# Where a turn computes the score rows of the next image: keys half or logits half

## The chip, the cores and the metric

The kernel runs on one core of a Trainium2 chip. The metric is the time of one execution on the device in microseconds (us), as the median of several runs. The engines are called TensorE (PE in the rows, its weight loads PEld), VectorE (DVE), ScalarE (ACT), GpSimd (POOL) and SyncE (SP, which issues all DMAs).

## What is computed

Eight images of 256 channels and 1024 pixels pass two attention layers. Layer 0 has 32 channels of queries and keys and no scale; layer 1 has group norm (32 groups), 256 channels and a projection:

```python
# layer 0, for each image, x: 256 x 1024
q = Wq x + bq; k = Wk x + bk; v = Wv x + bv            # q, k: 32 x 1024
x = gamma * v softmax(q^T k)^T + x
# layer 1
h = group_norm(x); q, k, v = q_w h + q_b, k_w h + k_b, v_w h + v_b
x = x + proj_w (v softmax(q^T k / 16)^T) + proj_b
```

## The kernel before

**Three matmuls for one.** Most operands are kept as a high and a low part, both in the type fp32r, and a product is high x high, high x low and low x high (`three`, L595, whose matmuls have the lines L596 to L598). ScalarE or GpSimd makes the high part, DVE or GpSimd the low part.

**Tiles.** An image has eight tiles of 128 pixels. In layer 0 a tile is handled twice. A *scores* tile (`scores`, L600, matmuls at L606) has query pixels in the partitions: DVE takes the maximum of its rows (L1058), and ScalarE the exponential with the row's sum (L841, in place). After all eight of an image ScalarE takes the logarithm of the sums (`log_sums`, L844), DVE makes -max - log(sum) of it, split in two (`shifts`, L1081), TensorE turns that into two rows (`move_shift`, L630), and ScalarE copies these to two extra rows of the query operand (`shift_rows`, L848). A *keys* tile (`keys`, L609, matmuls at L616) then has key pixels in the partitions and comes out shifted, so that one exponential (L817) gives finished probabilities; keys tile 0 waits for the shift rows. In layer 1 a *logits* tile (`logits`, L619) has its maximum, exponential, inverse sum and scaling in one pass (L1060, L1061, L820, L1067, L834). Each probability tile is split (ScalarE L831 or L834, DVE L1075 or L1078) and goes into a value product two steps later: twelve matmuls of 512 columns into four banks of PSUM slots 2 and 3 (`values`, L747). The value product needs the values' high and low parts. Those of layer 1 come from `value1` tiles (TensorE L672, DVE L987 to L991, ScalarE L858, GpSimd L504), each for two tiles of pixels; tile 3 of them serves value products 6 and 7.

**Slots.** Every tile that is no value product goes into a slot of `ring`. In the turns below only slots 0 and 1 are used, in strict alternation in TensorE's order, so each tile waits until the tile two before it has been read (`wait_read`, L583; `reader`, L248). The two small group-norm products share the slot of the fourth layer-0 value tile, so who takes that slot next waits for their readers too.

**Turns and steps.** `STEPS` is an order written by hand. The first two images have lists of their own. Then `turn(i)` for i = 2 to 7 has 16 steps: steps 0 to 7, the keys half, make the keys tiles of image i, and steps 8 to 15, the logits half, the logits tiles of image i - 1. Around them stand the preparations of image i + 1 (qk, scores, value0, shift) and of layer 1 of image i - 1 (query, value1); image i + 2 is split for its projections (`split_x`: high part on ScalarE, low part on DVE). Step s also has the value product of the tile of step s - 2, so that of steps 0 and 1 belongs to tiles 6 and 7 of the turn before. Turns 2 to 6 have a next image, turn 7 has none.

**The order within a step.** TensorE fills the step's tile, then `early`, then the first banks of the value product (one bank in the keys half, two in the logits half), then `sides`, the other banks, and `late`. ScalarE goes through tile, early, sides, high part of the logits, late, `log`, `split_x`. DVE takes a logits tile's maximum, then the low part of the tile before it (in front of the maximum for the tiles in `LOW_FIRST`, logits tile 7 among them), then the side work, the inverse, `x_lo_mid`, the other sides and late, `shifts`, statistics and `x_lo_end`. At step 10 DVE first evacuates the four banks of layer 0 (L1108). Each engine's queue is in program order, and a wait in it holds all that is behind it.

Of the kernel before, what the change touches and what calls it, by code (L numbers as in the profile page):

```python
# [34 lines left out]
class Step:  # L35
# [6 lines left out]
    def __init__(self, tile=None, values=None, banks_first=2, slots=(0, 1)):  # L42
        self.tile, self.values, self.banks_first, self.slots = tile, values, banks_first, slots
        self.early, self.sides, self.late = [], [], []
        self.early_log = self.log = self.shifts = self.hidden = self.hidden_lo = self.split_x = self.x_lo_mid = self.x_lo_end = None
        self.statistics = self.evacuate = self.evacuate_at_once = None
        self.take_weights = self.keep_values = self.opening = self.rest = self.low_first = False
        self.early_in_front = False
        self.hidden_mid = None
# [30 lines left out]
def tiles(kind, image, ks):  # L80
    return [(kind, image, k) for k in ks]
# [74 lines left out]
def turn(i):  # L156

    steps = [Step() for _ in range(2 * TILES)]
    has = lambda image: 0 <= image < IMAGES
    for s, step in enumerate(steps):  # L160
        if s < TILES and has(i):
            step.tile = ("keys", i, s)
        if s >= TILES and has(i - 1):
            step.tile = ("logits", i - 1, s - TILES)
        back = (s - 2) % (2 * TILES)
        layer, image = back // TILES, i - back // TILES - (s < 2)
        if has(image):
            step.values = (layer, image, back % TILES)
        if s < TILES:
            step.banks_first = 1  # L170
    if has(i + 1):
        steps[0].late = tiles("qk", i + 1, (0,))
        steps[3].banks_first = 0
        steps[3].sides = tiles("qk", i + 1, (1,))
        for k, s in enumerate((4, 5, 6, 7)):
            steps[s].early = tiles("scores", i + 1, (k,))
        for k, s in enumerate((8, 9, 11, 12)):
            steps[s].late = tiles("scores", i + 1, (4 + k,))
        for m, s in enumerate((9, 11, 12, 13)):
            steps[s].sides = tiles("value0", i + 1, (m,))  # L180
        steps[12].log = steps[13].shifts = i + 1
        steps[14].sides = tiles("shift", i + 1, (0,))
    if has(i - 1):
        for m, s in enumerate((4, 5)):
            steps[s].sides = tiles("query", i - 1, (m,))
        for m, s in enumerate((6, 7, 8)):
            steps[s].sides = tiles("value1", i - 1, (m,))
        last = steps[14] if has(i + 1) else steps[9]
        last.late += tiles("value1", i - 1, (3,))
        steps[1].hidden = steps[2].hidden_lo = i - 1  # L190
    if has(i + 1):
        steps[11].statistics, steps[12].statistics = ((i, 0),), ((i, 1),)
        steps[13].sides += tiles("norm", i, (0,))
        steps[13].late += tiles("norm", i, (1,))
    else:
        steps[10].statistics = (i, 0), (i, 1)
        steps[12].early, steps[12].late = tiles("norm", i, (0,)), tiles("norm", i, (1,))
        steps[12].hidden = steps[13].hidden_lo = i
        for m, s in enumerate((14, 15)):
            steps[s].late = tiles("query", i, (m,))  # L200
    if has(i + 2):
        steps[13].split_x, steps[13].x_lo_end, steps[14].x_lo_mid = i + 2, (i + 2, 0), (i + 2, 1)
    return steps
# [82 lines left out]
def build(nc, x, wqk_t, bqk, bk0, wv0_t, bv0, gamma, norm_w, norm_b, wq, bq, wk, bk, wv, bv, wp_t, bp,  # L286
          ident, group, y):
    with ExitStack() as ctx:
        def sb(name, shape, dt=F32):
            return ctx.enter_context(nc.sbuf_tensor(name, shape, dt))  # L290
# [27 lines left out]
        shift = sb("shift", [P, TILES])  # L318
# [618 lines left out]
        def _(dve):  # L937
# [3 lines left out]
            def link(ins):  # L941
                links[0] += 1
                ins.then_inc(S["link"], 1)
                dve.wait_ge(S["link"], links[0])
# [101 lines left out]
            def opening():  # L1046
                shifts(0)
                for m in range(2):
                    key_part(("qk", 1, m))
                for m in range(2):  # L1050
                    query_part(("qk", 1, m))
# [17 lines left out]
            def prob_lo(tile):  # L1069
                kind, i, k = tile  # L1070
                p = TILE_NO[tile]
                hi, lo, src = pt_hi[p % PT], pt_lo[p % PT], prob[:, p % PROBS]
                dve.wait_ge(S["p_hi"], p + 1)
                if kind == "keys":
                    V.tensor_tensor(lo[:], src, hi[:].bitcast(F32), ALU.subtract).then_inc(S["p_split"], 1)  # L1075
                else:
                    dve.wait_ge(S["inv_ready"], i * TILES + k + 1)
                    V.scalar_tensor_tensor(lo[:], src, row_inv[:, k % 2:k % 2 + 1], hi[:].bitcast(F32), ALU.mult,  # L1078
                                           ALU.subtract).then_inc(S["p_split"], 1)

            def shifts(i):  # L1081
                dve.wait_ge(S["log_ready"], i + 1)
                link(V.tensor_tensor(shift[:], neg_max0[:], log_sum0[:], ALU.subtract))
                link(V.tensor_copy(shift_pair[:, :, 0], shift[:]))
                V.tensor_tensor(shift_pair[:, :, 1], shift[:], shift_pair[:, :, 0].bitcast(F32),
                                ALU.subtract).then_inc(S["shift_ready"], 1)
# [36 lines left out]
            def follow(entry):  # L1123
                if entry[0] == "keys":
                    prob_lo(entry)
                elif entry[0] == "scores":
                    row_max(entry)
                elif entry[0] == "norm":
                    norm(entry)
                else:  # L1130
                    project_lo(entry)
# [3 lines left out]
            for now in STEPS:  # L1135
                if now.opening:
                    opening()
                    continue
                logits = now.tile and now.tile[0] == "logits"
                if now.evacuate:  # L1140
                    evacuate(*now.evacuate)
                if pending and not (logits and now.tile not in LOW_FIRST):
                    prob_lo(pending)
                    pending = None
                if logits:
                    row_max(now.tile)
                early_norm = [entry for entry in now.early if entry[0] == "norm"]
                for entry in early_norm:
                    norm(entry)
                if pending:  # L1150
                    prob_lo(pending)
                if now.take_weights:
                    take_weights()
                if now.hidden_lo is not None:
                    split_hidden(now.hidden_lo)
                for entry in now.early:
                    if entry not in early_norm:
                        follow(entry)
                if now.early_log is not None:
                    shifts(now.early_log)  # L1160
                first = [entry for entry in now.sides if entry[0] in ("qk", "norm", "bias")]
                if now.low_first:
                    prob_lo(now.tile)
                for entry in first:
                    if entry[0] != "norm":
                        follow(entry)
                if logits:
                    row_inverse(now.tile)
                    pending = now.tile
                    if now.x_lo_mid:  # L1170
                        split_x(*now.x_lo_mid)
                if now.evacuate_at_once:
                    evacuate(*now.evacuate_at_once)
                if now.tile and not logits and not now.low_first:
                    follow(now.tile)
                for entry in first:
                    if entry[0] == "norm":
                        follow(entry)
                for entry in now.sides + now.late:
                    if entry not in first:  # L1180
                        follow(entry)
                if now.keep_values:
                    keep_values()
                if now.shifts is not None:
                    shifts(now.shifts)
                for part in now.statistics or ():
                    statistics(*part)
                if now.x_lo_end:
                    split_x(*now.x_lo_end)
# [37 lines left out]
```

## Time and profile before

| what | us |
|---|---|
| median of three runs | 801.2 (801.15 to 802.32) |
| the profiled execution | 802.13 |
| its span, first to last instruction | 800.3 |
| TensorE busy | 784.6 |
| DVE busy | 550.7 |
| ScalarE busy | 468.1 |
| GpSimd busy | 163.7 |

The span is what the trace shows; the profiled execution's own time has 1.8 us around it. Busy time of TensorE is modelled at the ends of matmuls, which overlap: a matmul of 512 columns is shown as 0.39 us, and the next starts some 0.23 us after it. So starts are the better ruler: the distance between two starts is what TensorE needed or waited. The mean granted TensorE clock of the execution is 0.994 of full speed.

### The profile page before, as it was taken

To read this page: it belongs to the slowest core of one execution; us is meant where nothing else is said; L and a number is where in the kernel's file an instruction comes from. 1 tells how busy PE (TensorE), PEld (TensorE's weight loads), DVE (VectorE), ACT (ScalarE), POOL (GpSimd) and SP (SyncE) were. 2 spreads that over 40 slices of the span, in tenths; PEclk is the share of its full clock that TensorE was granted. 3 is DMA by queue.
4 is the path that set the end of the run, shared out by engine and by line. 5 is a ranking of instruction groups with operands and counts; after the bars stand their busy time and mean duration, and the time that the engine had idled before them with its cause. 6 is when DMAs were issued, how large, how long until landed. Compare 5 with 4: busy or idle time off the path is not lost.

```text
span 800.3 us, 9813 instructions
## 1 busy us (share of the span) xinstructions
PE 784.6 (98%) x3816; PEld 648.0 (81%) x3816; DVE 550.7 (69%) x790; ACT 468.1 (58%) x603; POOL 163.7 (20%) x147
## 2 busy tenths in 40 slices
PE   9889999999999999999999999999999999999998
PEld 8668787887888878888788877888778888888886
DVE  5866767778568775787657876577856756385564
ACT  4875655568556675557645676455864556445343
POOL 4730061023100231002410042102301024101120
PEclk9999999999999999999999999999999999999999
DMA  6010010002000030001100011000100001000101
GB/s 185 0 54 1 1 53 1 1 2 105 1 1 1 0 106 1 1 1 52 54 1 1 0 53 53 2 0 1 53 1 1 0 1 53 1 0 1 53 1 52
DMA packets 10365, 18.98 MB, mean 24 GB/s; under 512 B 2128, under 2 KB 3920, under 8 KB 10320
## 3 DMA queue, kind: packets, MB, share of 16 engines
q1 hardware_dynamic: 10320, 18.36, 6.6%
q8 instruction: 30, 0.49, 0.3%
q14 instruction: 15, 0.12, 0.1%
HBM read 9.97 MB, written 8.39 MB: 23 GB/s over the span
## 4 chain that ended last, share of the span: by engine, by line
PE 86%; DVE 9%; ACT 3%; issue 1%; POOL 0%; ACTq 0%; DVEq 0%; POOLq 0%
PE ring L596 26%; PE ring L598 26%; PE ring L597 26%; PE ring L606 4%; PE ring L616 3%; DVE res L1111 2%; DVE h_lo L963 1%; DVE pt_lo L1075 1%; DVE q L1030 1%; PE ring L593 1%; ACT ring L841 1%; DVE k L1022 1%; DVE k L1023 1%; ACT prob L817 1%; DVE neg_max L1058 1%
## 5 line engine op out<-in xcount | busy, mean ns | idle before, releaser
L596 PE MATMUL ring<-pt_hi,v_hi 128*128 128x512 f32 x480 | 190.1, 396 | 0.1
L598 PE MATMUL ring<-pt_hi,v_lo 128*128 128x512 f32 x480 | 188.8, 393 | 0.0
L597 PE MATMUL ring<-pt_lo,v_hi 128*128 128x512 f32 x480 | 188.6, 393 | 0.0
L820 ACT ACTIVATE prob<-ring,neg_max 128x1024 f32<-128x1024 f32 x64 | 71.5, 1117 | 157.1 <-DVE neg_max L1061 157.1
L1060 DVE TENSOR_REDUCE neg_raw<-ring 128x1 f32<-128x1024 f32 x64 | 78.1, 1221 | 59.4 <-PE ring L598 59.2
L504 POOL TENSOR_TENSOR v_lo<-v_f,v_hi 128x512 fp32r<-128x512 f32 x28 | 37.7, 1347 | 386.9 <-ACT v_hi L858 386.9
L598 PEld LDWEIGHTS ring<-pt_hi,v_lo 128*128 128x128 f32 x480 | 90.7, 189 | 20.1
L596 PEld LDWEIGHTS ring<-pt_hi,v_hi 128*128 128x128 f32 x480 | 90.6, 189 | 19.1 <-issue 1.6
L597 PEld LDWEIGHTS ring<-pt_lo,v_hi 128*128 128x128 f32 x480 | 90.9, 189 | 17.8
L1075 DVE TENSOR_TENSOR pt_lo<-prob,pt_hi 128x1024 fp32r<-128x1024 f32 x64 | 82.1, 1283 | 32.9 <-ACT pt_hi L831 32.7
L1058 DVE TENSOR_REDUCE neg_max<-ring 128x1 f32<-128x1024 f32 x64 | 77.6, 1222 | 36.8 <-PE ring L606 36.8
L1078 DVE SCALAR_TENSOR_TENSOR pt_lo<-prob,row_inv,pt_hi 128x1024 fp32r<-128x1024 f32 x64 | 83.0, 1297 | 15.0 <-ACT pt_hi L834 15.0
L841 ACT ACTIVATE ring<-ring,neg_max 128x1024 f32<-128x1024 f32 x64 | 69.5, 1085 | 40.7 <-DVE neg_max L1058 40.6
L596 PE MATMUL ring<-h_hi,query_hi 128*128 128x512 f32 x224 | 88.0, 393 | 0.0
L597 PE MATMUL ring<-h_lo,query_hi 128*128 128x512 f32 x224 | 87.5, 391 | 0.0
L598 PE MATMUL ring<-h_hi,query_lo 128*128 128x512 f32 x224 | 87.5, 391 | 0.0
L817 ACT ACTIVATE prob<-ring 128x1024 f32<-128x1024 f32 x64 | 65.3, 1020 | 36.4 <-PE ring L616 36.2
L834 ACT ACTIVATE pt_hi<-prob,row_inv 128x1024 fp32r<-128x1024 f32 x64 | 73.8, 1153 | 11.0 <-DVE row_inv L1067 10.8
L831 ACT CAST pt_hi<-prob 128x1024 fp32r<-128x1024 f32 x64 | 67.2, 1051 | 5.3
L606 PE MATMUL ring<-k,q 96*128 96x512 f32 x128 | 42.2, 416 | 9.2 <-ACT ring L841 5.8
L598 PEld LDWEIGHTS ring<-h_hi,query_lo 128*128 128x128 f32 x224 | 42.1, 188 | 8.9
L596 PEld LDWEIGHTS ring<-h_hi,query_hi 128*128 128x128 f32 x224 | 42.1, 188 | 8.9 <-DVE v_lo L1010 0.2
(167 smaller groups left out, 1346.5 us busy)
## 6 DMA issues: line engine op xcount, KB each, us to landing
out_y<-res SPq DMA_DIRECT2D x32, 256.0 KB, 2.2
x_in<-in_x SPq DMA_DIRECT2D x7, 1024.0 KB, 4.9
x_in<-in_x SPq DMA_DIRECT2D x2, 512.0 KB, 5.6
h_f<-in_wv_t SPq DMA_DIRECT2D x1, 256.0 KB, 3.7
res<-in_wq SPq DMA_DIRECT2D x1, 256.0 KB, 6.0
res<-in_wk SPq DMA_DIRECT2D x1, 256.0 KB, 6.3
res<-in_wv SPq DMA_DIRECT2D x1, 256.0 KB, 6.5
res<-in_wp_t SPq DMA_DIRECT2D x1, 256.0 KB, 6.0
```

The source lines that it names most:

```text
L596: mm(out, w_hi, m_hi, start=first, stop=False)
L597: mm(out, w_hi, m_lo, start=False, stop=False)
L598: return mm(out, w_lo, m_hi, start=False, stop=last)
L606: last = mm(out[:, cols], q4[i % 2][0:96, rows], k4[i % 2][0:96, cols], start=True, stop=True)
L817: activation(prob[:, p % PROBS], ring[:, slot], ACT.Exp).then_inc(S["keys_exp"], 1)
L820: activation(prob[:, p % PROBS], ring[:, slot], ACT.Exp, bias=neg_max[:, k % 2:k % 2 + 1], accum_out=row_sum[:, k % 2:k % 2 + 1]).then_inc ...
L834: activation(pt_hi[p % PT][:], prob[:, p % PROBS], ACT.Identity, scale=row_inv[:, k % 2:k % 2 + 1]).then_inc(S["p_hi"], 1)
L841: activation(ring[:, slot], ring[:, slot], ACT.Exp, bias=neg_max0[:, k:k + 1], accum_out=row_sum0[:, k:k + 1]).then_inc(S["scores_exp"], 1)
L1058: V.tensor_reduce(neg_max0[:, k:k + 1], src, AX_X, ALU.max, negate=True).then_inc(S["scores_max"], 1)
L1060: link(V.tensor_reduce(neg_raw[:, k % 2:k % 2 + 1], src, AX_X, ALU.max, negate=True))
L1075: V.tensor_tensor(lo[:], src, hi[:].bitcast(F32), ALU.subtract).then_inc(S["p_split"], 1)
L1078: V.scalar_tensor_tensor(lo[:], src, row_inv[:, k % 2:k % 2 + 1], hi[:].bitcast(F32), ALU.mult, ALU.subtract).then_inc(S["p_split"], 1)
```

## The change

In `turn(i)`, before, scores tiles 0 to 3 of the next image stand in steps 4 to 7 and tiles 4 to 7 in steps 8, 9, 11 and 12. After, tile 0 stands in step 7 and tiles 1 to 7 in steps 8 to 14. The logarithm moves from step 12 to the end of step 14, DVE's `shifts` from the end of step 13 to step 15, between the maximum and the inverse of the logits tile, and TensorE's shift from between the banks of step 14 to the end of step 15. The last value1 tile, which follows the shift, moves with it from the end of step 14 to the end of step 15. In step 13, scores tile 6 stands ahead of the second group-norm product on all engines, and ahead of the split of image i + 2. Nothing else moves, and no instruction is added or left out.

```diff
--- before.py
+++ after.py
@@ -42,7 +42,7 @@
     def __init__(self, tile=None, values=None, banks_first=2, slots=(0, 1)):
         self.tile, self.values, self.banks_first, self.slots = tile, values, banks_first, slots
         self.early, self.sides, self.late = [], [], []
-        self.early_log = self.log = self.shifts = self.hidden = self.hidden_lo = self.split_x = self.x_lo_mid = self.x_lo_end = None
+        self.early_log = self.log = self.shifts = self.shifts_first = self.hidden = self.hidden_lo = self.split_x = self.x_lo_mid = self.x_lo_end = None
         self.statistics = self.evacuate = self.evacuate_at_once = None
         self.take_weights = self.keep_values = self.opening = self.rest = self.low_first = False
         self.early_in_front = False
@@ -172,20 +172,19 @@
         steps[0].late = tiles("qk", i + 1, (0,))
         steps[3].banks_first = 0
         steps[3].sides = tiles("qk", i + 1, (1,))
-        for k, s in enumerate((4, 5, 6, 7)):
-            steps[s].early = tiles("scores", i + 1, (k,))
-        for k, s in enumerate((8, 9, 11, 12)):
-            steps[s].late = tiles("scores", i + 1, (4 + k,))
+        steps[7].early = tiles("scores", i + 1, (0,))
+        for k, s in enumerate((8, 9, 10, 11, 12, 13, 14)):
+            steps[s].late = tiles("scores", i + 1, (1 + k,))
         for m, s in enumerate((9, 11, 12, 13)):
             steps[s].sides = tiles("value0", i + 1, (m,))
-        steps[12].log = steps[13].shifts = i + 1
-        steps[14].sides = tiles("shift", i + 1, (0,))
+        steps[14].log = steps[15].shifts_first = i + 1
+        steps[15].late = tiles("shift", i + 1, (0,))
     if has(i - 1):
         for m, s in enumerate((4, 5)):
             steps[s].sides = tiles("query", i - 1, (m,))
         for m, s in enumerate((6, 7, 8)):
             steps[s].sides = tiles("value1", i - 1, (m,))
-        last = steps[14] if has(i + 1) else steps[9]
+        last = steps[15] if has(i + 1) else steps[9]
         last.late += tiles("value1", i - 1, (3,))
         steps[1].hidden = steps[2].hidden_lo = i - 1
     if has(i + 1):
@@ -1164,6 +1163,8 @@
                 for entry in first:
                     if entry[0] != "norm":
                         follow(entry)
+                if now.shifts_first is not None:
+                    shifts(now.shifts_first)
                 if logits:
                     row_inverse(now.tile)
                     pending = now.tile
```

## Rows read from the trace of the kernel before

**Rows 1.** The page: busy time of TensorE, and two groups of instructions.

```profile
PE 784.6 (98%) x3816; PEld 648.0 (81%) x3816; DVE 550.7 (69%) x790; ACT 468.1 (58%) x603; POOL 163.7 (20%) x147
...
L1060 DVE TENSOR_REDUCE neg_raw<-ring 128x1 f32<-128x1024 f32 x64 | 78.1, 1221 | 59.4 <-PE ring L598 59.2
...
L504 POOL TENSOR_TENSOR v_lo<-v_f,v_hi 128x512 fp32r<-128x512 f32 x28 | 37.7, 1347 | 386.9 <-ACT v_hi L858 386.9
```

**Rows 2.** Waits of TensorE: in total, times, longest us.

```profile
PE ring L606 <- ACT ring L841: 5.8, 7, 2.1
PE ring L606 <- DVE q L1030: 3.3, 6, 0.7
```

**Rows 3.** Timeline of turn 4, steps 4 and 5: start us, us, engine, line.

```profile
384.34 0.70 PE L606 MATMUL ring<-k,q 96*128 96x512 f32 x2 [0.47 <-DVE q L1030]
...
389.73 1.28 DVE L1005 SCALAR_TENSOR_TENSOR query_lo<-ring,query_b,query_hi 128x1024 fp32r<-128x1024 f32 x1 [2.08 <-ACT query_hi L861]
...
390.44 0.63 PE L616 MATMUL ring<-q,k 98*128 98x512 f32 x2
...
391.07 0.73 PE L606 MATMUL ring<-k,q 96*128 96x512 f32 x2
```

**Rows 4.** Timeline of turn 4, step 10.

```profile
424.15 2.72 DVE L1108 SCALAR_TENSOR_TENSOR x<-ring,gamma_s,x 128x512 f32<-128x512 f32 x4
...
428.26 0.39 PE L596 MATMUL ring<-h_hi,query_hi 128*128 128x512 f32 x1
...
428.39 1.12 ACT L820 ACTIVATE prob<-ring,neg_max 128x1024 f32<-128x1024 f32 x1 [2.93 <-DVE neg_max L1061]
...
429.41 0.19 ACT L820 ACTIVATION_READ_ACCUMULATOR prob<-ring,neg_max 128x1 f32 x1
```

**Rows 5.** Timeline: a scores tile of step 12, a logits tile of step 15.

```profile
442.52 0.63 PE L606 MATMUL ring<-k,q 96*128 96x512 f32 x2
...
445.46 0.19 ACT L841 ACTIVATION_READ_ACCUMULATOR ring<-ring,neg_max 128x1 f32 x1
...
460.53 0.39 PE L596 MATMUL ring<-pt_hi,v_hi 128*128 128x512 f32 x1
...
463.37 0.19 ACT L820 ACTIVATION_READ_ACCUMULATOR prob<-ring,neg_max 128x1 f32 x1
```

**Rows 6.** Timeline of turn 4, steps 13 to 15.

```profile
450.11 0.28 PE L688 MATMUL ring<-spread,group_s 128*128 128x2 f32 x2
...
450.24 1.98 ACT L802 CAST x_hi<-x_in 128x1024 fp32r<-128x1024 f32 x2
...
456.14 1.00 ACT L851 CAST q<-ring 2x1024 fp32r<-2x1024 f32 x1
...
457.17 1.15 ACT L834 ACTIVATE pt_hi<-prob,row_inv 128x1024 fp32r<-128x1024 f32 x1
```

**Rows 7.** Timeline: turn 4's first value product and norm, last value1, turn 5's first value product.

```profile
367.80 0.39 PE L596 MATMUL ring<-pt_hi,v_hi 128*128 128x512 f32 x1
...
375.65 2.38 ACT L807 ACTIVATE h_hi<-x,norm_c,norm_a 128x1024 fp32r<-128x1024 f32 x2
...
456.35 0.28 PE L596 MATMUL ring<-wpv_hi,h_hi 128*128 128x258 f32 x1
...
459.61 1.61 POOL L504 TENSOR_TENSOR v_lo<-v_f,v_hi 128x512 fp32r<-128x512 f32 x1 [42.80 <-ACT v_hi L858]
...
463.72 0.39 PE L596 MATMUL ring<-pt_hi,v_hi 128*128 128x512 f32 x1
```

**Rows 8.** Windows of TensorE: us, busy (count), granted clock, DMA share, GB/s.

```profile
24.00:26.00 2.00, 0.96 (x4) 1.00 0.00 0
26.00:28.00 2.00, 1.64 (x6) 0.68 0.00 0
28.00:30.00 2.00, 2.00 (x6) 0.50 0.00 0
...
120.00:122.00 2.00, 0.31 (x2) 1.00 0.04 14
```

## The prediction

> **What bounds the kernel now.** I read the page first: TensorE's records cover 98% of the span, and no other engine reaches 70% [rows 1]. So the order of TensorE's work is the time, and only its gaps can be won. The view of waits says which gaps come before a scores tile: 5.8 us for ScalarE's release of a ring slot and 3.3 us for the query half that DVE writes, over the whole kernel [rows 2]. Then I read the timeline of turn 4 (367 to 463 us), which stands for turns 2 to 6. In its keys half TensorE waits before the first three scores tiles: 0.47 us at 384.34, with the record drained about 0.63 us between the end of the work before and the start; 391.07 comes 0.63 us after the keys pair at 390.44, where a pair of matmuls needs 0.47, and it starts just as DVE ends the query's low part at 389.73 + 1.28 = 391.01 [rows 3]. The third, at step 6, is like the second. After a wait the pair lasts 0.73 instead of 0.63, a refill of 0.1 [rows 3, 5]. In the second half of the turn TensorE has no wait that the timeline shows. There the reader should see not gaps but how near the chains are that end just in time.
>
> **Units.** A value product and a keys pair together take 463.72 - 460.53 = 3.19 us, so a value product or a logits tile (twelve matmuls of 512 columns) takes 2.72 and a pair 0.47. A scores tile's slot is free 445.65 - 442.52 = 3.13 us after its first matmul starts: row maximum, exponential, accumulator read. A logits tile's slot is free 463.56 - 460.53 = 3.03 us after TensorE goes on to the next product [rows 5], if DVE and ScalarE are idle then. A row maximum is 1.22 us, a low split 1.28, a high split 1.15, the shift's copy 1.00 [rows 1, 3, 6].
>
> **What the change wins.** The work is the same; it only moves. Three scores tiles leave steps 4 to 6 of the keys half. Step 4 then has the query projection where the first scores tile was. It takes the slot of the second half of qk, so it waits for the same DVE release, but 0.68 us of value product lie before it instead of behind it (its matmuls come after the first bank); that covers the 0.63. The query's slot is asked for again after 2.04 + 0.47 + 0.68 = 3.19 us, and today the release comes 391.01 - 390.44 = 0.57 us into the keys pair, which stands 2.04 us behind the query's end: after 2.6 us, so there is no new wait. I take 0.63 + 2 x 0.16 for the waits and 3 x 0.09 for the refills: 1.2 us a turn, 6.1 us over five turns.
>
> **What it costs in step 10.** Ring slots 0 and 1 alternate. With a scores tile between logits 2 and logits 3, logits 3 takes the slot of logits 2 and not that of a scores tile long read. Logits 2's exponential is late, because DVE evacuates four banks first (424.15 to 426.87) and only then takes the maximum: the exponential and its accumulator read end at 429.60, and logits 3, at 428.26 now, would be due at 428.26 + 0.47 = 428.73 [rows 4]. Wait 0.9 us, 4.6 over five turns. The later tiles of steps 11 and 12 keep the pattern of today (a scores tile after the value projection), so they cost nothing.
>
> **What it costs from step 13 to the next turn.** I count u from 450.11, where the second group mean's matmul starts [rows 6]. Up to there nothing but the 0.47s changes.
> - Scores 6 stands at u 0 to 0.47, its maximum on DVE at 0.67 to 1.9, its slot's release at 3.13. DVE reads the second group mean behind that maximum, at 2.1. Logits 6 now takes the slot in which that mean lies, so it starts at 2.15 instead of 0.6.
> - On ScalarE the split of the image after next is behind the scores exponential: 3.15 to 5.1 instead of from 450.24 - 450.11 = 0.13 (1.98 us for both halves [rows 6]). DVE's low half is behind its first half, 4.2 to 5.4, and logits 6's maximum behind that, 5.4 to 6.65. Its exponential is read at 8.25.
> - TensorE: logits 6 to 4.95, values 4 to 7.65, scores 7 to 8.1. Logits 7 takes logits 6's slot: starts 8.3, ends 11.05. Values 5 to 13.8.
> - DVE: low split 5 to 8.15, inverse 8.25, x low half to 9.55, scores 7's maximum to 10.8, low split 6 to 12.05 (it stands in front of maximum 7), maximum 7 and its shift to 13.6, the three small operations of `shifts` to 14.15. So the shift's matmuls wait, 14.2 to 14.7, and the last value projection waits for logits 7's exponential: 14.95 to 16.4.
> - ScalarE: high split 7 at 15.2 to 16.3, then the shift's copy 16.3 to 17.3. Keys 0 of the next turn waits for it: 17.35 to 17.8.
> - The last value projection is what is later still. Value product 6, the first of the next turn, needs its low part. Today that is POOL's and ends at 461.22, 4.87 us after the projection's first matmul at 456.35, with 2.5 us to spare before 463.72 [rows 7]. Now the projection is the last thing in front of keys 0: 14.95 + 4.87 = 19.82, and value product 6 starts at 19.9. Without waits it would start at 463.72 - 450.11 + 2 x 0.47 = 14.55. Cost: 5.3 us a turn.
>
> Turn 6 has no image to split; the same steps give 19.05 there, 4.5 us. Sum 4 x 5.3 + 4.5 = 25.7 us. Refills after some four of these waits a turn: about 0.3 each turn, 1.5 us.
>
> In POOL's queue the norm's coefficients and the normalised image stand behind this split, so they too come later, to about 1.5 and 4 us into the next turn's step 0. ScalarE wants them only at 375.65, 7.85 us after the turn's first value product at 367.80 [rows 7], so this is hidden. No DMA is moved, and SP's queue waits for events that only move with the turn.
>
> POOL's split took 1.61 us at 459.61, beside a DVE low split out of SBUF, and that is in the 4.87. The Trainium skill (SBUF — State Buffer, Who interferes with whom) says that VectorE with two SBUF inputs and GpSimd exclude each other from a shared port pair. The split falls beside DVE's low split 7 again, so by the rule the sum stays as it is, and the row agrees with a split that is held up; without it the stall would be about 0.26 us less a turn, from the mean of 1.35 us of the 28 such splits [rows 1].
>
> **The clock.** In the first image the granted clock was 0.68 in 26 to 28 us and 0.50 in 28 to 30, after TensorE had been busy 0.96 us of the 2 from 24 to 26 in several short waits; that is the 1.2 GHz level, and it costs 2 x 0.32 + 2 x 0.50 = 1.6 us of work. At 120 to 122 us TensorE was busy only 0.31 of 2 us, in one wait, and the clock stayed at 1.00 [rows 8]. The end of a turn after the change has waits of 0.9 and 2.05 us with one pair between them, more than either. I expect the clock to fall after most of them, not all: 3.5 of 5, 5.7 us. Bounds: none, 0, and all five, 8.2.
>
> **Sum.** -6.1 + 4.6 + 25.7 + 1.5 + 5.7 = +31.4 us on the profiled execution's 802.1 us (span 800.3). That is 0.9 above the median of 801.2, so the forecast for the median is 832.6.
>
> **Rivals.**
> - The clock does not fall: 832.6 - 5.7 = 827. For it: the wait at 120 us did not bring it down. Against it: twice as much idle in one place.
> - Only the late last projection counts, because DVE and ScalarE catch up in some way that my order of their queues misses. Then keys 0 starts on time and value product 6 waits 4.87 - 1.45 - 0.47 = 2.95 us: 5 x 2.95 + 4.6 - 6.1 = +13, about 814. Against it: the queues are in program order, and each of the steps above is one place in it.
> - Faster: the projection's low part is in time after all. It decides by the 4.87 us chain: where that chain and the shift's copy were over within 1.9 us of the projection's start (its own 1.45 and the keys pair), only step 10's wait would stand against the win: -6.1 + 4.6 = -1.5, and about -6 if that were hidden too: 795 to 800. POOL's split alone takes 1.61 of these [rows 7], with DVE's add and ScalarE's high part in front of it, so value product 6 would have to do without the low part, which its wait in the code excludes.
> - No change: wins and waits cancel. It needs all of the turn's end to cost under 0.5 us a turn; nothing speaks for it.
>
> **How the numbers follow.** The forecast with three to five falls of the clock 0.62; clock stays or falls once or twice 0.18; projection alone 0.10; faster 0.03; no change 0.02; still slower, by waits that go on into the keys half or a fall elsewhere, 0.05. Range: from 816, just above the projection alone, to 840, the sum with all five falls (835) and 5 us for waits that I place too early. A measurement of this kernel tells 0.2% (1.6 us) from no change. Faster 0.03, same 0.02, slower 0.95.
>
> **What would show it.** In the changed profile: no wait before scores 0 in step 7 and none by L1030 in the keys half; a wait of 0.9 us before logits 3 on L820; one of 1.5 before logits 6 on DVE's L1098; keys 0 (L616) waiting on L851 about 0.9 us; and one of about 2 us before the first value product of a turn, on POOL's L504, five times. Turns 2 to 6 take about 101 to 103 us instead of 463.72 - 367.80 = 95.9, and the granted clock falls at the start of most. The prediction is wrong if value product 6 does not wait, if the turn's end overlaps its waits otherwise, or if turn 7 or the first two images change by more than a few tenths.

## The result, and the profile after

The changed kernel takes 831.47 us (median of four runs, 831.16 to 834.15) where the kernel before takes 801.76 in the same comparison: ratio 1.0371, 95% interval 1.035 to 1.0392. The forecast was 832.6 us, in a range of 816 to 840. Of all the executions reported below, one of the changed kernel with the group mean first ran at a mean granted clock of 0.555 and took 1303.5 us; it is left out of that kernel's median, which is of the other three. Line numbers in the profile after are one lower than before in all that follows `turn`, since the edit shortens it (L596 has become L595, L504 L503); in the experiments they are shifted by a few lines too.

The page after: the span, the busy time of the engines, and the value products' and logits tiles' first matmuls with the idle time of TensorE in front of them.

```profile
span 829.4 us, 9808 instructions
...
PE 791.9 (95%) x3816; PEld 652.5 (79%) x3816; DVE 548.4 (66%) x790; ACT 468.9 (57%) x603; POOL 173.0 (21%) x147
...
L595 PE MATMUL ring<-pt_hi,v_hi 128*128 128x512 f32 x480 | 192.4, 401 | 8.8 <-POOL v_lo L503 8.7
...
L595 PE MATMUL ring<-h_hi,query_hi 128*128 128x512 f32 x224 | 89.0, 397 | 10.6 <-DVE var_eps L1097 6.8
```

The work is the same 3816 matmuls, and the span is 29.1 us longer than the 800.3 of before. The view of TensorE's waits, after (in total, times, longest us):

```profile
PE ring L595 <- POOL v_lo L503: 8.7, 5, 1.8
PE ring L595 <- DVE var_eps L1097: 6.8, 5, 1.4
PE ring L605 <- ACT ring L840: 5.8, 7, 2.1
PE ring L615 <- ACT q L850: 4.7, 6, 0.9
PE ring L595 <- ACT prob L819: 3.8, 5, 0.8
...
PE ring L605 <- DVE q L1029: 0.4, 1, 0.4
```

Against [rows 2]: the scores tiles' wait for DVE's query half has gone from 3.3 us to 0.4 (the first image's), which is the change's gain. The 5.8 us on ScalarE's slot release are exactly those of before: they lie in the first images. Four waits are new, and each comes five times, once a turn (the sixth on L850, keys 0's wait for the shift rows, was there before, in the first images). Here they are in turn 4, first the one in step 10, then the turn's end (timeline: start, duration us, engine, line; in brackets idle time and what ended it):

```profile
376.36 0.80 PE L595 MATMUL ring<-pt_hi,v_hi 128*128 128x512 f32 x1 [1.74 <-POOL v_lo L503]
...
431.62 2.72 DVE L1107 SCALAR_TENSOR_TENSOR x<-ring,gamma_s,x 128x512 f32<-128x512 f32 x4
...
436.88 0.19 ACT L819 ACTIVATION_READ_ACCUMULATOR prob<-ring,neg_max 128x1 f32 x1
437.13 0.50 PE L595 MATMUL ring<-h_hi,query_hi 128*128 128x512 f32 x1 [0.76 <-ACT prob L819]
...
459.16 0.63 PE L605 MATMUL ring<-k,q 96*128 96x512 f32 x2
...
461.26 0.47 PE L595 MATMUL ring<-h_hi,query_hi 128*128 128x512 f32 x1 [1.36 <-DVE var_eps L1097]
...
462.18 1.99 ACT L801 CAST x_hi<-x_in 128x1024 fp32r<-128x1024 f32 x2
...
463.25 1.23 DVE L954 TENSOR_TENSOR x_lo<-x_in,x_hi 128x1024 fp32r<-128x1024 f32 x1 [2.14 <-ACT x_hi L801]
...
467.03 0.19 ACT L819 ACTIVATION_READ_ACCUMULATOR prob<-ring,neg_max 128x1 f32 x1
...
467.27 0.50 PE L595 MATMUL ring<-h_hi,query_hi 128*128 128x512 f32 x1
...
472.94 0.64 PE L634 MATMUL ring<-ident_r,shift_pair 128*2 128x128 f32 x8
...
473.66 0.39 PE L595 MATMUL ring<-wpv_hi,h_hi 128*128 128x258 f32 x1
...
475.07 1.00 ACT L850 CAST q<-ring 2x1024 fp32r<-2x1024 f32 x1
...
476.22 0.70 PE L615 MATMUL ring<-q,k 98*128 98x512 f32 x2 [0.84 <-ACT q L850]
...
477.02 1.58 POOL L503 TENSOR_TENSOR v_lo<-v_f,v_hi 128x512 fp32r<-128x512 f32 x1 [52.74 <-ACT v_hi L857]
...
478.66 0.80 PE L595 MATMUL ring<-pt_hi,v_hi 128*128 128x512 f32 x1 [1.74 <-POOL v_lo L503]
```

Read it with the prediction's u, whose zero is scores 6 at 459.16. Logits 6 starts at u 2.10 (forecast 2.15), DVE's low half of the next-but-one image at 4.09 (4.2), logits 6's slot is free at 8.06 (8.25), logits 7 starts at 8.11 (8.3), the shift at 13.78 (14.2), the last value projection at 14.50 (14.95), keys 0 at 17.06 (17.35), value product 6 at 19.50 (19.9). The turn, from value product 6 to value product 6, takes 478.66 - 376.36 = 102.3 us where it took 95.9 [rows 7].

The clock, in windows of TensorE (us, busy, granted clock, DMA share, GB/s) at the ends of turns 2 and 4, after:

```profile
274.00:276.00 2.00, 0.55 (x2) 1.00 0.00 0
276.00:278.00 2.00, 2.00 (x10) 1.00 0.00 0
...
478.00:480.00 2.00, 1.34 (x3) 0.60 0.00 0
480.00:482.00 2.00, 2.00 (x6) 0.55 0.00 0
```

It fell to the 1.2 GHz level at the ends of four of the five turns (not of turn 2, whose waits are the same). A fall takes away 2 x 0.40 + 2 x 0.45 = 1.7 us of clock, but part of it falls into the wait itself, where it costs nothing: turns 4 and 5, which begin at the low level, take 102.3 us, and turn 3, which does not, 100.9. So a fall costs about 1.4 us there, 1.5 in turn 6, and the whole 1.7 in turn 7.

The terms, in the profiled executions, beside the forecast:

| term | forecast us | measured us |
|---|---|---|
| step 10, five turns | 4.6 | 4.7 (5 x 0.94 between start and due start) |
| turn's end, u 0 to value product 6, less 14.55 | 4 x 5.3 + 4.5 = 25.7 | 4 x 4.95 + 4.47 = 24.3 |
| clock | 5.7 | 2 x 1.4 + 1.5 + 1.7 = 6.0 |
| gains and refills | -6.1 + 1.5 = -4.6 | -4.7 (what is left) |
| turns 2 to 6 and the start of turn 7 | 31.4 | 30.3 |
| the first images | 0 | -1.2 |
| span | 31.4 | 29.1 |

The first images come 1.2 us sooner in this execution although nothing in them is changed. 1.0 us of it is there after the first 6 us, in the preparation: from 4 to 6 us TensorE runs 20 matmuls in this execution and 11 in that of the kernel before. It is a difference between executions, not one that the change makes.

### The profile page after: what moved, and what is told of

Read it like the earlier page. It is cut to its first block, busy times and chain, and to the rows that moved or that the text cites. A ratio compares the mean times of both kernels' runs of the same rounds, so it can differ in the third digit from the quotient of the medians.

```text
span 829.4 us, 9808 instructions
## 1 busy us (share of the span) xinstructions
PE 791.9 (95%) x3816; PEld 652.5 (79%) x3816; DVE 548.4 (66%) x790; ACT 468.9 (57%) x603; POOL 173.0 (21%) x147
## 4 chain that ended last, share of the span: by engine, by line
PE 78%; DVE 10%; ACT 7%; issue 3%; POOL 1%; ACTq 0%; DVEq 0%; POOLq 0%
PE ring L595 24%; PE ring L596 23%; PE ring L597 23%; PE ring L615 3%; PE ring L605 3%; DVE neg_max L1057 2%; ACT prob L819 2%; DVE neg_raw L1059 2%; ACT prob L816 2%; DVE x L1107 2%; ACT ring L840 1%; ACT pt_hi L830 1%; PE ring L592 1%; POOL v_lo L503 1%; DVE v_f L989 1%
## 5 line engine op out<-in xcount | busy, mean ns | idle before, releaser
L595 PE MATMUL ring<-pt_hi,v_hi 128*128 128x512 f32 x480 | 192.4, 401 | 8.8 <-POOL v_lo L503 8.7
L596 PE MATMUL ring<-pt_lo,v_hi 128*128 128x512 f32 x480 | 190.2, 396 | 0.0
L819 ACT ACTIVATE prob<-ring,neg_max 128x1024 f32<-128x1024 f32 x64 | 71.5, 1117 | 148.3 <-DVE neg_max L1060 148.3
L503 POOL TENSOR_TENSOR v_lo<-v_f,v_hi 128x512 fp32r<-128x512 f32 x28 | 37.6, 1342 | 422.1 <-ACT v_hi L857 422.1
L595 PEld LDWEIGHTS ring<-pt_hi,v_hi 128*128 128x128 f32 x480 | 92.1, 192 | 29.8 <-POOL v_lo L503 10.9
L596 PEld LDWEIGHTS ring<-pt_lo,v_hi 128*128 128x128 f32 x480 | 92.2, 192 | 18.2
L595 PE MATMUL ring<-h_hi,query_hi 128*128 128x512 f32 x224 | 89.0, 397 | 10.6 <-DVE var_eps L1097 6.8
L596 PE MATMUL ring<-h_lo,query_hi 128*128 128x512 f32 x224 | 87.6, 391 | 0.0
L595 PEld LDWEIGHTS ring<-h_hi,query_hi 128*128 128x128 f32 x224 | 42.0, 188 | 23.0 <-ACT prob L819 7.4
L596 PEld LDWEIGHTS ring<-h_lo,query_hi 128*128 128x128 f32 x224 | 42.1, 188 | 8.5
```

The source lines that it names most:

```text
L595: mm(out, w_hi, m_hi, start=first, stop=False)
L596: mm(out, w_hi, m_lo, start=False, stop=False)
L819: activation(prob[:, p % PROBS], ring[:, slot], ACT.Exp, bias=neg_max[:, k % 2:k % 2 + 1], accum_out=row_sum[:, k % 2:k % 2 + 1]).then_inc ...
```

## The experiments

Each edit is in `turn` unless said; times are medians, and ratios are to the kernel before on the same chip.

**The turn's end alone.** The kernel before with the logarithm, the shift and the last value1 tile late (and, as in the change, DVE's `shifts` between maximum and inverse):

```diff
-        steps[12].log = steps[13].shifts = i + 1
-        steps[14].sides = tiles("shift", i + 1, (0,))
+        steps[14].log = steps[15].shifts_first = i + 1
+        steps[15].late = tiles("shift", i + 1, (0,))
-        last = steps[14] if has(i + 1) else steps[9]
+        last = steps[15] if has(i + 1) else steps[9]
```

> The kernel before with one part of the change: the logarithm, the shift and the last value1 tile late (end of step 14, step 15), all scores tiles where they were. My theory: the order at the turn's end makes most of the loss by itself. Logits 7 then ends some 2.3 us before the last value1 tile, its exponential, high split and the shift's copy make keys 0 wait 0.9 us, and value product 6 waits 2.0 us more for POOL's low part, since only 1.45 + 0.47 us lie between it and the 4.87 us chain: 2.9 us a turn, 14.5 us in five turns, and 1.6 us for each of some four falls of the clock: 823 us. Rival: the two scores tiles of steps 13 and 14 make the loss, by holding up DVE and ScalarE; then the late shift alone costs little, under 5 us, and the time is 802 to 807.

Measured: 821.7 us, ratio 1.0261 (1.0244 to 1.0277). Its waits of TensorE:

```profile
PE ring L596 <- POOL v_lo L504: 8.7, 5, 1.7
...
PE ring L616 <- ACT q L851: 4.7, 6, 0.9
```

The two waits at the start of the next turn are those of the full change, to 0.1 us. So the late shift and value1 tile make 20 of the 29 us by themselves, the clock's falls among them; the rival is out. The other 9 come with the moved scores tiles, net of their gain. Turns in which the clock did not fall say the same: 95.9 us before, 98.7 here (turns 5 and 6), 100.9 in the changed kernel (turn 3). Of the 2.2 us between the last two, step 10 makes 0.9 and the gain takes off about 0.9, so by subtraction the scores tiles of steps 13 and 14 and the later group mean cost 2.2; they were not run alone.

**A scores tile in step 10 alone.** The kernel before with `enumerate((8, 9, 10, 12))` for `(8, 9, 11, 12)`.

> The kernel before with one scores tile (tile 6) moved from step 11 to step 10, nothing else. My theory: logits 3 then takes the slot of logits 2, whose maximum stands behind the evacuation in DVE's queue, and waits 0.9 us on L820 five times: 806.3 us, 4.6 more than before. Rival: the wait is taken out of slack later (step 11 has one pair less, and DVE and ScalarE are idle there), and the time is that of before within 1 us.

Measured: 808.62 us (806.65 to 809.42), ratio 1.0087 (1.0071 to 1.0102). Logits 3 of turn 5:

```profile
529.70 0.50 PE L596 MATMUL ring<-h_hi,query_hi 128*128 128x512 f32 x1 [0.76 <-ACT prob L820]
```

The wait is the forecast one, in each of the five turns, and the rival is out. The median is 2.3 us above my figure. Of the 6.3 us between the profiled executions 5.2 are the edit's (five turns of 97.0 instead of 95.9 us), and 1.0 is a start of turn 2 that comes later. That is not the edit's work, and the trace shows where it arises, in the first images:

```profile
108.89 1.21 POOL L489 TENSOR_SCALAR res<-x,unit,bp_s 128x1024 f32<-128x1024 f32 x1
...
109.02 2.15 DVE L1075 TENSOR_TENSOR pt_lo<-prob,pt_hi 128x1024 fp32r<-128x1024 f32 x1 [1.18 <-ACT pt_hi L831]
```

In the kernel before the same two operations start at 108.93 and 109.04, and it is POOL's that takes 2.25 us and DVE's that takes 1.23. Here DVE's is the long one, its next operations are late, and TensorE waits 0.81 us in front of a query tile at 114.94 where it had no wait.

**The second group mean ahead of scores 6.** The changed kernel with:

```diff
-        steps[13].late += tiles("norm", i, (1,))
+        steps[13].late = tiles("norm", i, (1,)) + steps[13].late
```

> The changed kernel with the second group-norm product ahead of scores tile 6 in step 13 again, on all engines. The trace shows 6.8 us of waits on its reader (L1097) before logits 6. My theory, chains that overlap: DVE takes the maximum of logits 6 behind the low half of image i + 2 anyway, so that in turns 2 to 5 the wait only moves, from before logits 6 to before logits 7, which grows from about 0.1 to 1.5 us; only turn 6, which has no image to split, gains its 1.4 us: 830 us, 1.4 less than the changed kernel. Rival, waits that add: all 6.8 us are won, 824.7 us.

Measured: 833.44 us (median of three), ratio 1.0397 (1.0379 to 1.0414). Waits, and logits 7 of turn 4:

```profile
PE ring L595 <- ACT prob L819: 10.0, 9, 1.5
```

```profile
469.65 0.50 PE L595 MATMUL ring<-h_hi,query_hi 128*128 128x512 f32 x1 [1.54 <-ACT prob L819]
```

The wait on L1097, 6.8 us, is gone, and that on L819 has grown from 3.8 to 10.0 us, by 1.54 in each of turns 2 to 5. That is the overlap, and the rival with 824.7 is out. Turn 6, keys 0 to keys 0, went from 101.84 to 100.46 us, the 1.4 forecast. But the whole did not become 1.4 us faster. It measures 2 us slower, though the intervals of the two kernels overlap: in the profiled execution turns 2, 3 and 5 are 0.2 to 0.3 us longer, and turn 4 is 1.6 us longer, with the clock low for twice as long at its start. That the single, longer wait brings this about is not shown.

**Filling the wait.** The changed kernel with the first qk product in front of value product 6:

```diff
-        steps[0].late = tiles("qk", i + 1, (0,))
+        steps[0].early = tiles("qk", i + 1, (0,))
```

> The changed kernel with the first qk product of step 0 (six matmuls of 512 columns, 1.36 us) ahead of value product 6 instead of behind it, so that it falls into the wait for POOL. My theory: the wait before the value product shrinks from 1.99 to about 0.6 us, 1.36 x 5 = 6.8 us are won, and the clock, which fell at four of five turn ends, stays up, since the long wait is gone: another 6 us, 818 us. If the clock still falls (because the waits from the shift on count together): 824.7. Rival: value product 6 starts later by what qk takes, since POOL's chain and DVE's queue move too, and little is won: 830.

Measured: 823.44 us, ratio 1.0273 (1.0255 to 1.029), 8 us less than the changed kernel. Value product 6 at the start of turn 5, the waits in sum, and the windows around it:

```profile
477.05 0.50 PE L595 MATMUL ring<-pt_hi,v_hi 128*128 128x512 f32 x1 [0.35 <-POOL v_lo L503]
```

```profile
PE ring L595 <- POOL v_lo L503: 3.2, 5, 1.8
```

```profile
476.00:478.00 2.00, 1.65 (x7) 1.00 0.00 0
478.00:480.00 2.00, 2.00 (x11) 1.00 0.00 0
```

The wait shrinks from 1.74 to 0.35 us in turns 3 to 6; turn 7 has no qk product to put there and keeps its 1.8, which my 5 x 1.36 overlooked. The clock stays up at those four ends, where it fell at three in the changed kernel, and falls only at turn 7's start. From keys 0 of turn 2 to keys 0 of turn 7 it takes 495.7 us instead of 506.3, 10.6 less. Turn 3, which has the clock up in both kernels, shows what the wait and its refill are worth, 100.9 - 99.35 = 1.55 us; turns 4 to 6 gain some 3.0 each, so that a fall of the clock is worth about 1.45. The profiled execution as a whole gains less, 7.7 us, because keys 0 of turn 2 comes 2.9 us later in it, after first images that the edit does not touch. 1.2 of these are what the changed kernel's profiled execution had gained there by chance, and 1.7 are a fall of the clock behind the wait at 120 to 122 us, which I had taken for one that does not bring the clock down [rows 8]:

```profile
122.00:124.00 2.00, 1.98 (x6) 0.66 0.00 0
```

So the idle time at the turn's start is what brings the clock down, though not each time. In the profiled executions of the changed kernel and of the four here whose turns still begin behind two waits (tail_alone, norm_first, value1_in_14, norm_first_split_15) it fell at 18 of 25 ends; with the second wait cut to 0.35 us it fell at none of four. It need not be the wait for POOL: the next experiment has none, and the clock falls at four of its five ends.

**The value1 tile early, the shift still late.** The changed kernel with `steps[14].sides = tiles("value1", i - 1, (3,))` instead of the tile at the end of step 15.

> The changed kernel with the last value1 tile between the banks of step 14, so that it is early again; the shift stays at the end of step 15. My theory: POOL's low part was only the last to end of two chains that are nearly level. The wait on L504's successor (8.7 us) goes, but the tile takes DVE and ScalarE in step 14, holds up the high split of logits 6 and scores 7, and the shift's copy comes that much later: keys 0 waits 2 to 2.5 us instead of 0.9. Time within 3 us of the changed kernel: 829 to 832. Rival, the late projection is the whole cause of the turn end's loss: 8.7 us of waits and the 6.6 us of the clock are won, 816.

Measured: 831.24 us, ratio 1.0351 (1.0332 to 1.037). Its waits, and keys 0 of turn 5:

```profile
PE ring L617 <- ACT q L852: 9.2, 6, 1.9
...
PE ring L636 <- DVE shift_pair L1086: 2.8, 5, 1.4
PE ring L597 <- DVE v_f L991: 2.0, 4, 0.5
```

```profile
479.80 0.69 PE L617 MATMUL ring<-q,k 98*128 98x512 f32 x1 [1.71 <-ACT q L852]
```

No wait for POOL is left, and the time is the same: the shift's chain takes its place at once, with 1.71 us instead of 0.84 in front of keys 0 (I had expected 2 to 2.5), 0.24 to 1.36 in front of the shift, and, in turns 2 to 5, 0.5 in front of logits 7. Moving the late projection back alone mends nothing.

**DVE relieved in step 13.** The changed kernel with the group mean first, and the split of image i + 2 moved behind the turn's end:

```diff
-        steps[13].late += tiles("norm", i, (1,))
+        steps[13].late = tiles("norm", i, (1,)) + steps[13].late
-        steps[13].split_x, steps[13].x_lo_end, steps[14].x_lo_mid = i + 2, (i + 2, 0), (i + 2, 1)
+        steps[15].split_x, steps[15].x_lo_end = i + 2, (i + 2, 0)
+    if 2 < i < LAST:
+        steps[0].x_lo_end = i + 1, 1
```

> The changed kernel with the second group-norm product ahead of scores tile 6, and with the split of image i + 2 in step 15 (its second low half in step 0 of the next turn), so that neither holds up DVE in front of logits 6's maximum. My theory: with both gone the waits before logits 6 (1.36) and logits 7 (1.5 with the norm alone) both go and all that follows in the turn comes about 2 us earlier relative to the work, while keys 0 still waits 0.8 us for the shift's copy and value product 6 still 1.9 for POOL: about 2.1 us in turns 2 to 5 and 1.4 in turn 6, 10 us: 821, and 822 to 825 if the split in ScalarE's queue holds up keys 0. Rival: ScalarE and DVE pay for the split wherever it stands, so that the time stays within 3 us of the changed kernel.

Measured: 821.1 us (818.85 to 824.76), ratio 1.0216 (1.0187 to 1.0245). Its waits:

```profile
PE ring L597 <- POOL v_lo L505: 7.6, 5, 1.8
...
PE ring L617 <- ACT q L852: 4.6, 6, 0.8
PE ring L597 <- ACT prob L821: 3.8, 5, 0.8
PE ring L597 <- DVE res L1112: 2.6, 4, 0.7
```

Of the waits in front of logits 6 and 7 nothing is left; the 3.8 us on L821 are those of step 10. So the second group mean and the image's split together, but not the mean alone, held up the chain, as forecast; the split moved alone was not run. The size is less sure than the median looks. The four executions are two of 818.9 us, at a granted clock of 0.992, and one each of 823.3 and 824.8, at 0.988 and 0.985, and the profile is of the slowest, so that how often the clock fell makes part of the 10 us. Free of it are the turns of the profile that begin with the clock up, 99.2 us instead of 100.9. A new one of 0.65 us, four times, stands in step 2, where value product 0 waits for an evacuation that DVE now does behind the split's second half; I had not seen it.

**Only the largest of the waits.** The kernel before, the end of the turn untouched:

```diff
-        for k, s in enumerate((4, 5, 6, 7)):
+        for k, s in enumerate((5, 6, 7)):
             steps[s].early = tiles("scores", i + 1, (k,))
+        steps[7].late = tiles("scores", i + 1, (3,))
```

> The kernel before with the scores tiles of the keys half in steps 5, 6, 7 and, as a second tile at the end of it, 7 again, instead of 4 to 7; the logits half and the turn's end untouched. My theory: only the wait before scores 0 in step 4 (0.63 us and a refill of 0.1) can be won without touching a chain that ends just in time, and step 7 has room: its second tile has 3.13 us until its slot is asked for again. 0.7 x 5 = 3.5 us are won: ratio 0.9956. Rival: query 0 in step 4 now takes the slot of qk and waits for the same DVE release instead: no change within 1 us.

Measured: 798.73 us where the kernel before has 802.67 in these rounds, ratio 0.9954 (0.9937 to 0.9971), forecast 0.9956. The waits on DVE's query half fell from 3.3 to 0.7 us (the row below), and a turn from 95.9 to 95.3.

```profile
PE ring L607 <- DVE q L1031: 0.7, 1, 0.7
```

**Scores behind the bank.** From there, scores tiles of steps 5 and 6 as the first of `sides`, with DVE's maximum kept in front of the keys tile's low split (`scores_first` lets DVE's loop take such a tile with qk, norm and bias).

> two_in_step7 with the scores tiles of steps 5 and 6 behind the first bank of the value product instead of ahead of it (DVE still takes their maximum ahead of the low split of the keys tile). They wait 0.16 to 0.2 us, and a refill of 0.1, for the query's low part, which is done 2.6 us after the query's end; behind the bank they start 3.19 us after it. My theory: both waits go, 2 x 0.25 x 5 = 2.5 us on top of the 3.5 of two_in_step7: ratio 0.9925. Rival: the scores tile's row maximum then holds up the low split on DVE, or query 1 and the keys tile after it wait for slots instead, and the ratio stays at 0.9955 or rises.

Measured: 799.45 us (797.55 to 800.71), ratio 0.9967 (0.9954 to 0.998): no gain on two_in_step7; the intervals overlap. Keys 5 and query 1 of turn 4:

```profile
386.70 0.63 PE L620 MATMUL ring<-q,k 98*128 98x512 f32 x2
...
387.43 1.03 ACT L821 ACTIVATE prob<-ring 128x1024 f32<-128x1024 f32 x1 [1.46 <-PE ring L620]
...
388.50 0.50 PE L600 MATMUL ring<-h_hi,wqq_hi 128*128 128x512 f32 x1
```

Query 1 starts 1.80 us after keys 5, where 0.47 + 0.68 + 0.47 = 1.62 us of work lie between: it needs that tile's slot, whose exponential ends at 388.46. The rival was right, and the wait has only changed its place.

**Two banks in step 7.** `steps[7].banks_first = 2` on top.

> behind_bank with two banks of the value product instead of one ahead of the value1 tile of step 7, which waits some 0.17 us (and a refill) for the exponential of keys 7. My theory: 0.68 us more lie in front of it, the wait goes, 0.28 x 5 = 1.4 us: ratio 0.991. Rival: logits 0 then asks for that tile's slot after 1.36 + 0.47 us where its reading takes some 1.7, and the wait comes back there: the ratio of behind_bank.

Measured: 796.88 us, ratio 0.9941 (0.9929 to 0.9953); the wait before the value1 tile of step 7 is gone, and turns take 94.97 us instead of behind_bank's 95.24.

**Two banks in steps 5 to 7.** `steps[s].banks_first = 2` for s = 5 and 6 too. The edit against the kernel before, without the line that sets the new field `scores_first` to `False`:

```diff
-        for k, s in enumerate((4, 5, 6, 7)):
-            steps[s].early = tiles("scores", i + 1, (k,))
+        for k, s in enumerate((5, 6)):
+            steps[s].sides = tiles("scores", i + 1, (k,))
+            steps[s].scores_first = True
+            steps[s].banks_first = 2
+        steps[7].early = tiles("scores", i + 1, (2,))
+        steps[7].banks_first = 2
+        steps[7].late = tiles("scores", i + 1, (3,))
...
-            steps[s].sides = tiles("query", i - 1, (m,))
+            steps[s].sides = steps[s].sides + tiles("query", i - 1, (m,))
...
-            steps[s].sides = tiles("value1", i - 1, (m,))
+            steps[s].sides = steps[s].sides + tiles("value1", i - 1, (m,))
...
-                first = [entry for entry in now.sides if entry[0] in ("qk", "norm", "bias")]
+                first = [entry for entry in now.sides if entry[0] in ("qk", "norm", "bias") or
+                         entry[0] == "scores" and now.scores_first]
```

> behind_bank_two_banks with two banks of the value product ahead of the side work in steps 5 and 6 too. In behind_bank the waits of 0.16 us before scores went, but query 1 and value1 0 then waited 0.18 us for the exponential of the step's keys tile, which is read 1.75 us after the keys pair starts, with 0.47 + 0.68 + 0.47 = 1.62 us of work in front. My theory: another bank (0.68 us) covers that, and the two waits and their refills go: 2 x 0.28 x 5 = 2.8 us, ratio 0.9906 where behind_bank_two_banks had 0.9941. Rival: keys 7, which now has 3.27 us of work in front where the scores tile's slot takes 3.13, or the value1 tiles, which POOL gets later, wait instead: 0.994.

Measured: 796.15 us, ratio 0.9931 (0.9913 to 0.9948), turns of 94.66 us. The page of this kernel:

```profile
span 793.5 us, 9808 instructions
...
PE 780.4 (98%) x3816; PEld 648.9 (82%) x3816; DVE 549.4 (69%) x790; ACT 468.9 (59%) x603; POOL 165.6 (21%) x147
```

The two waits are gone; one of 0.14 us is left in front of scores 2 in step 7, which is a little sooner after value1 0 than before. The gain over the last version is 0.3 us a turn instead of the 0.56 forecast, and the intervals of the two overlap, so that it is the whole against the kernel before, 0.7%, that is shown. It has the lowest time of the versions here.

## Why the prediction was right

**What bounds the kernel.** TensorE's order is the time, as said: every us of the loss is a wait of TensorE or a stretch at its lower clock, and the versions that won did it by removing waits of 0.1 to 0.6 us.

**The win** was right: the waits before scores tiles are gone, and two_in_step7 shows the largest of them by itself, 3.5 us forecast for ratio 0.9956, and 0.9954 measured. I had put all three waits down as won; of the gaps in front of side work in the keys half one (the value1 tile of step 7) grew from 0.18 to 0.28 us, which I had not listed.

**Step 10** was right to 0.1 us in the changed kernel and shown alone.

**The turn's end** was right as a chain, place by place, and 0.35 us a turn too long, since I added a little for each handover on DVE, where one operation starts 0.08 to 0.09 us before the record of the last one ends (four such places between u 5 and 12). What the experiments add is how the parts hang together: the shift and the projection alone make two thirds of the loss, with their falls of the clock; two chains, the shift's copy and POOL's low part, end within a fraction of a us of each other in what they cost, so that taking one away wins nothing; and the mean's wait in front of logits 6 lies in the shadow of the image's split, so that taking it away alone wins nothing either. The rival of a late projection as the only cause fails on value1_in_14. The time alone would not have ruled it out: its 814 left out the clock, and with the 5.7 us of the sum it would have stood near 820, inside the range.

**POOL.** Its split took 1.58 us, beside DVE's low split, as assumed, and the coefficients behind it cost TensorE nothing.

**The clock** fell after four of five turns where I had counted 3.5 from two rows of the kernel before, which is a guess that came near and not a rule; a fall cost 1.4 to 1.7 us where I had 1.6. qk_first shows the cause: with the wait cut to a fifth the clock stayed up at all four ends where that was done.

**The signs of being wrong.** One of them came: turn 7 or the first images were to change by no more than a few tenths. Behind value product 6, turn 7 is 1.7 us longer, and that is its fall of the clock, which the term for the clock holds. The first images differ by 1.2 us, and by 1.0 the other way in step10_alone, with the same instructions in the same order. So I should have allowed for this much between executions, and it says nothing against the mechanism.

**The rivals.** No change, faster and the projection alone are out. "The clock does not fall" is out for four ends of five, and holds for one with the same waits.

## What to carry to other kernels

Where a kernel's bounding engine works through a hand-written order, an item may be moved only as far as the chains behind it have slack: write for each the time from its start to its last reader, and compare it with the work left in front of that reader. A wait in a ring of slots is mended by putting more work between two uses of the slot, not by moving the tile to another half where another slot is short. And before taking one wait away, look for the chain that ends next: here two that were level and one in another's shadow made single repairs worth nothing.

## What was not expected of the hardware

A tiny operation of POOL can be held for almost as long as DVE's large one beside it lasts. Two rows of the timeline after:

```profile
479.20 1.22 DVE L1074 TENSOR_TENSOR pt_lo<-prob,pt_hi 128x1024 fp32r<-128x1024 f32 x1 [1.72 <-ACT pt_hi L830]
...
479.34 1.14 POOL L470 TENSOR_TENSOR norm_a<-rstd,nw_s 128x2 f32<-128x2 f32 x1
```

A product of two columns takes 1.14 us and ends at 480.48, just behind DVE's low split at 480.42; in the kernel before the same operation took 0.19 or 0.20 us in seven of its eight executions, that of turn 4 among them, and 1.15 in one. The Trainium skill (SBUF — State Buffer, Who interferes with whom) calls the port pair of DVE and GpSimd an exclusive lock; this trace agrees, with 0.95 us of holding up for 0.19 us of work. DVE can be the one that is held: in step10_alone above it is, by 0.9 us. Which of the two waits does not follow from the distance of their starts: in the kernel before and in norm_first_split_15 DVE's starts 0.11 us behind POOL's, and in the one POOL's takes 2.25 us, in the other DVE's 2.17.

The same waits do not always bring the clock down: at the end of turn 2 of the changed kernel TensorE was busy 0.55 us of 2 and the clock stayed at 1.00, at four other ends it fell. Behind the wait at 120 to 122 us it fell in the profile of qk_first and in none of the other eleven. In the kernel with the turn's end alone it fell after three of the five (windows of 10 us: granted clock 0.83, 0.83 and 0.66 at turns' ends, 1.00 at two).
